# Masks of two groups of columns in one VectorE operation, in a graph attention layer with a 0/1 adjacency matrix

## The reference

```python
xt = jnp.einsum('ni,hio->hno', x, W)
src = jnp.einsum('hnf,hf->hn', xt, a[:, :out_f])
dst = jnp.einsum('hnf,hf->hn', xt, a[:, out_f:])
e = jax.nn.leaky_relu(src[:, :, None] + dst[:, None, :], 0.2)
e = jnp.where((adj_matrix > 0)[None, :, :], e, -jnp.inf)
h_prime = jnp.einsum('hij,hjf->hif', jax.nn.softmax(e, axis=2), xt)
x = _layernorm(x + h_prime.transpose(1, 0, 2).reshape(n, heads * out_f), axis=-1)
```

## Time and profile before

| what | value |
|---|---|
| median of 3 runs | 2133.12 us (2133.09 to 2134.42) |
| span of the profiled execution | 2129.9 us |
| TensorE matmul busy | 2068.3 us, 97% |
| VectorE busy | 2037.9 us, 96% |
| ScalarE busy | 1991.4 us, 93% |
| chain that ended last | TensorE 85%, ScalarE 7%, VectorE 4% |

### The profile page before, as it was taken

One profiled execution on the slowest core, in us unless ns is written; L12 is line 12 of the kernel. 1 busy time (PEld: TensorE's weight loads), 2 busy tenths in 40 slices (PEclk: granted clock), 3 DMA queues, 4 the chain that ended last, 5 costly groups with the idle time before them and its releaser, 6 DMA issues.

```text
span 2129.9 us, 76758 instructions
## 1 busy us (share of the span) xinstructions
PE 2068.3 (97%) x34256; PEld 2045.3 (96%) x34256; DVE 2037.9 (96%) x2147; ACT 1991.4 (93%) x2019; POOL 203.9 (10%) x179
## 2 busy tenths in 40 slices
PE   7779999999999999999999999999999999999997
PEld 5569999999999999999999999999999999999997
DVE  4999999999999999999999999999999999999887
ACT  4588999999999999999999999999999999999995
POOL 0200000000200102000020002001020001201000
PEclk9999999999999999999999999999999999999998
DMA  9999777666666766676666766767666766534321
GB/s 309 372 368 383 270 259 251 228 216 212 212 219 220 260 219 216 206 245 221 218 218 218 260 217 196 230 212 255 216 219 216 246 224 215 185 83 122 87 53 41
DMA packets 237208, 469.37 MB, mean 220 GB/s; under 512 B 14736, under 2 KB 23952, under 8 KB 236880
## 3 DMA queue, kind: packets, MB, share of 16 engines
q1 hardware_dynamic: 232672, 448.58, 63.9%
q0 software_dynamic: 4080, 15.73, 2.2%
q10 hardware_dynamic: 128, 0.13, 0.0%
HBM read 438.83 MB, written 25.56 MB: 218 GB/s over the span
## 4 chain that ended last, share of the span: by engine, by line
PE 85%; ACT 7%; DVE 4%; DMA 1%; issue 1%; SPq 0%; POOL 0%; DVEq 0%; ACTq 0%; POOLq 0%
PE acc L997 80%; ACT big L504 7%; PE tp L961 4%; DVE AT L679 1%; DVE big L684 1%; DVE big L686 1%; DVE AT L678 1%; PE acc L913 0%; DMA AT<-in_x_dram 0%; DMA raw<-in_adj_dram 0%; PE acc L923 0%; DMA v_parts<-big 0%; DVE nat L624 0%; SPq L321 0%; PE tp L951 0%
## 5 line engine op out<-in xcount | busy, mean ns | idle before, releaser
L504 ACT ACTIVATE big<-big,d_all 128x1024 int8<-128x1024 f32 x1776 | 1872.4, 1143 | 36.7 <-PE acc L997 36.6
L997 PE MATMUL acc<-big 128*128 128x130 f16 x32768 | 1889.1, 220 | 8.8 <-DVE big L708 7.9
L997 PEld LDWEIGHTS acc<-big 128*128 128x128 fp8e5 x32768 | 1878.0, 98 | 11.7 <-issue 10.3
L701 DVE SCALAR_TENSOR_TENSOR big<-big,AT 128x1024 uint32<-128x1024 uint32 x512 | 625.5, 1222 | 26.3 <-ACT big L504 24.5
L708 DVE SCALAR_TENSOR_TENSOR big<-AT,big 128x1024 uint32<-128x1024 uint32 x512 | 625.1, 1221 | 3.0
L693 DVE TENSOR_SCALAR big<-big,d_all 128x1024 uint8<-128x1024 f32 x272 | 204.6, 752 | 0.0
L624 DVE TENSOR_SCALAR nat<-raw 128x2048 fp8e4<-128x2048 int32 x128 | 176.7, 1381 | 2.9 <-DMA raw<-in_adj_dram 2.6
L626 DVE TENSOR_SCALAR nat<-raw 128x2048 uint8<-128x2048 int32 x128 | 177.5, 1387 | 0.0
L439 POOL TENSOR_TENSOR wden<-big,ab 128x16 f32<-128x16 f32 x31 | 68.3, 2205 | 885.0 <-DVE big L734 885.0
L635 DVE SCALAR_TENSOR_TENSOR AT<-AT,tp 128x1024 uint32<-128x1024 uint32 x112 | 136.4, 1217 | 0.1
L961 PE MATMUL tp<-ident,nat 128*128 128x128 f32 x896 | 116.8, 273 | 0.0
(11 more groups left out here) (67 smaller groups left out, 403.1 us busy)
## 6 DMA issues: line engine op xcount, KB each, us to landing
raw<-in_adj_dram SPq DMA_DIRECT2D x256, 1024.0 KB, 6.2
big<-v_parts SPq DMA_DIRECT2D x512, 260.0 KB, 3.6
v_parts<-big SPq DMA_DIRECT2D x16, 1040.0 KB, 6.1
big<-s_rows SPq DMA_DIRECT2D x32, 512.0 KB, 4.5
AT<-in_x_dram SPq DMA_DIRECT2D x16, 512.0 KB, 8.9
big<-in_x_dram POOLq DMA_DIRECT2D x8, 1024.0 KB, 8.0
out_dram<-big POOLq DMA_DIRECT2D x7, 1024.0 KB, 5.9
out_dram<-big SPq DMA_DIRECT2D x2, 384.0 KB, 2.7
```

The source lines that it names most:

```text
L504: return nc.scalar.activation(sgn[:, g % NB, b, :], srow[:, h % 2, :], ACT.Sign, bias=dflat[:, r:r + 1], scale=-1.0)
L701: nc.vector.scalar_tensor_tensor(out=word(sgn, g % NB), in0=word(sgn, g % NB), scalar=EDGE[plane], in1=edges(g), op0=ALU.bitwise_and, op1= ...
L997: return nc.tensor.matmul(acc[:, k, o:o + 2 * VO], m[:, g % NB, b, t * P:(t + 1) * P], Vr[:, v:v + 2 * VO], start=opens, stop=False, skip_ ...
```

## The change

In all passes but the first, the positive masks of groups g and g + 1 (g even) are made by one operation over 2048 words instead of two over 1024, and so are the negative masks. Both stand at the even group. The compares of both groups come ahead of the pair's positive masks, and converts stay at the odd group, which is now behind the pair's negative masks. The merge waits for the positive masks of the pair just issued and for the negative masks of all pairs before.

```diff
+            def masks_of_two(n, g, plane, cmps, kept):
+                for k in kept:
+                    dve.wait_ge(at_done, k)
+                dve.wait_ge(cmp_done, cmps)
+                dve.wait_ge(sgn_done, n + 2)
+                of = words_of(sgn, g % NB)
+                nc.vector.scalar_tensor_tensor(out=of, in0=of, scalar=EDGE[plane], in1=edges_of(g),
+                                               op0=ALU.bitwise_and, op1=ALU.bitwise_and).then_inc(pos_done, 2)
+
+            def rest_of_two(n, g, plane, kept):
+                for k in kept:
+                    dve.wait_ge(at_done, k)
+                dve.wait_ge(sums_done, n + 2)
+                dve.wait_ge(pos_done, n + 2)
+                nc.vector.scalar_tensor_tensor(out=words_of(neg, g % NB), in0=edges_of(g), scalar=EDGE[plane], in1=words_of(sgn, g % NB),
+                                               op0=ALU.bitwise_and, op1=ALU.bitwise_xor).then_inc(neg_done, 2)
...
-                z = (g - j) % NG
-                dve.wait_ge(pos_done if z == 0 else neg_done, n + 1 if z == 0 else n - z + 5)
+                dve.wait_ge(pos_done, n - n % 2 + 2)
+                dve.wait_ge(neg_done, n + 4 + n % 2)
...
-                        if not made:
-                            masks_of(n, g, plane, (0 if first else compared_ahead(c)) + compared(g, h, first, not more), last[g])
+                        single = first and h == 0
+                        ahead = 0 if first else compared_ahead(c)
+                        if single and not made:
+                            masks_of(n, g, plane, ahead + compared(g, h, first, not more), last[g])
+                        if not single and g % 2 == 0:
+                            if scalar_blocks(g, first, not more) < B:
+                                compares(n, g, h, scalar_blocks(g, first, not more))
+                            if scalar_blocks(g + 1, first, not more) < B:
+                                compares(n + 1, g + 1, h, scalar_blocks(g + 1, first, not more))
+                            masks_of_two(n, g, plane, ahead + compared(g + 1, h, first, not more), (last[g], last[g + 1]))
                         if ended and g == 1:
                             high(p, 0)
-                        by_scalar = scalar_blocks((g + 1) % NG, first and h > 0, not more)
-                        if by_scalar < B and not made:
+                        by_scalar = scalar_blocks((g + 1) % NG)
+                        if single and by_scalar < B and not made:
                             compares(n + 1, g + 1, h, by_scalar)
...
-                        if not made:
+                        if single and not made:
                             rest_of(n, g, plane, last[g])
+                        if not single and g % 2 == 0:
+                            rest_of_two(n, g, plane, (last[g], last[g + 1]))
```

More of the change, by code:

```diff
@@ L185, in word, with words_of, edges_of @@
             return t[:, n].rearrange("p b i -> p (b i)").bitcast(u32)
+        def words_of(t, n):
+            return t[:, n:n + 2].rearrange("p n b i -> p (n b i)").bitcast(u32)
+        def edges_of(g):
+            return AT[:, g:g + 2].rearrange("p g b s i -> p (g b s i)")
         def edges(g):
```

## The result

The changed kernel takes 2278.47 us (median of 4 runs, 2274.31 to 2280.29), against 2133.11 beside it: 1.068 of the time before (1.0668 to 1.0694). The prediction was 2225, with 2178 to 2250 as its range; the direction was right, and the time lies 53 us above the forecast and 28 above the range. The profiled execution spans 2277.8 us instead of 2129.9, so 147.9 us are to be explained.

What follows compares the result with a forecast made beforehand. TensorE was taken as the floor, its steady passes without gaps. Stalls of 3.2 us in 24 passes (77), 6 in the last four and 9 in passes 1 to 3 sum to 92: from 2133.1 to 2225 us, range 2178 to 2250.

Steps and rivals of the forecast that it cites:

- it can't overlap by 0.09 and starts 0.03 after its end: VectorE's masks or merge directly behind the masks they wait for: 0.12 us each, seven times a pass, 0.8 us.
- Three such pairs: 1.1 us a pass.: Pairs with a merge at groups 6, 10 and 14: TensorE stands 0.38 us at each one's first negative mask.
- Rival A: The merge pairs just fit, with 0.1 less in each hiding their stall; 2.1 us a pass, 2198 us; chance 0.17.
- "0.6 us" where a pass begins: Group 0: the first high, now behind the double masks, lets TensorE start at 12.97 against arrival at 12.36.
- Groups 2 and 3, "1.5 us": The lows hold back these signs: negative masks usable at 23.52, wanted at 22.05, so TensorE stands 1.5 us.
- Passes 1 to 3, "9, from 3 to 14": ScalarE itself is the chain there; about 2 us stall where a pass begins, few long loops; 3 us a pass.
- "Sum 6" for the last passes: Last four passes: 0.6 us entering pass 28, then 1.9 at each later beginning, 5.7 together; other pairs in time.

Runs made afterwards that it cites:

- e1: The changed kernel with a pair's compares moved ahead of the convert before them, away from the masks; 2265.38 us, 1.0622 of before.
- e5: e1, with the merge no longer waiting for the pair just issued where it doesn't touch it; 2238.62 us, 1.0496 of before.
- e11: The kernel before, with even groups' positive masks also waiting for the odd group's signs, from group 2 and pass 4 on; 2166.31 us, 1.016.
- e13: e11 with the operation that weighs the sums (group 8) cut to 1 column of 64; 2166.25 us, 1.0153 of before.
- e17: The kernel before, with only group 14's positive mask also waiting for group 15's signs, from pass 4 on; 2156.93 us, 1.0115.
- e18: e11 with the two adds at group 12 cut to 1 column of 64; 2157.31 us, 1.0116 of before.
- e12: The changed kernel with single masks in passes 0 to 3 and at groups 0 and 1 of every pass; 2249.45 us, 1.0545 of before.
- e4: The changed kernel with single masks in the whole first chunk (passes 0 to 3), pairs from pass 4 on; 2251.15 us, 1.0554 of before.
- e3: The changed kernel with a pair's negative masks again two operations, one behind the other at the same place; 2264.98 us, 1.062 of before.
- e9: e8 with the pairing left out in passes 1 to 3 and at groups 0 and 1 of every pass; 2156.04 us, 1.0111 of before.
- e10: The changed kernel with compares ahead of the convert, merge at the odd group, single masks in passes 0 to 3 and groups 0 to 3; 2181.11 us, 1.0229.
- e8: The kernel before, with only a pair's negative masks made in one operation, at the odd group ahead of the convert; 2191.84 us, 1.0277.

## Why the prediction was wrong, by its own steps

Sign and places were right: five stalls a pass, at the first `high` and at groups 2, 6, 10 and 14, the double mask at 2.29 us (2.28 predicted), VectorE's busy time unchanged. Sizes were not. The sum was 92 us and 147.9 were measured: 21 of the 56 missing lie in passes 1 to 3, 29 in passes 4 to 27, 6 at the end. Two things failed in the steady passes: the price of a wait of VectorE for itself, and the lateness that one pair hands to the next, which stood in the sum as nothing.

*"it can't overlap by 0.09 and starts 0.03 after its end".* The loss of overlap was right, the 0.03 was mis-sized. Rows 7 are of operations on 6 and 3 elements a partition; for the merge behind a double mask it is 0.20, for a mask behind a mask 0.13. With 0.17 more for the merge the working comes out right where nothing else is late: at group 6 it gives 0.38 + 0.17 = 0.55, and 0.39 + 0.16 = 0.55 were measured. A wait of 0.23 behind the compares, which the change puts right ahead of the masks, wasn't in the sum. Taken off, the compares' waits give back 13 us (e1) and the merges' 27 (e5), thereof 10 and 24 in passes 4 to 27. Of the 24, 0.12 x 4 x 24 = 11.5 were in the sum.

*"Three such pairs: 1.1 us a pass."* 0.39 + 0.52 + 0.71 and three times 0.16: 2.1. The growth from 6 to 14 is the queue: 0.13 and 0.33 us beyond the signs, by the table above, so 0.55 + 0.13 = 0.68 and 0.55 + 0.33 = 0.88, as measured (0.52 + 0.16 and 0.71 + 0.16). The working took each pair for itself, and excludes this. Rival A, a loop 0.1 shorter that just fits, had the sign of the error wrong.

*"0.6 us" where a pass begins.* The working starts the masks 0.15 us behind the last sign. They started 1.0 behind (1084.27 to 1085.29), since VectorE was still at the work of the pair before and at the compares. The stall was 1.07 + 0.16 instead of 0.6; that it didn't grow by the whole 0.9 is because TensorE came later too, by the larger stall at group 14 (0.87 instead of 0.38). e11, e13, e17 and e18 show this mechanism apart: the slack of a pair isn't its own, and late work is passed on down the queue.

*Groups 2 and 3, "1.5 us".* 1.14 + 0.16 = 1.30. This one was smaller, since TensorE came later to it, by the larger stall ahead of it. e1 and e12 show the trade: what is taken from one shows at the other.

*Passes 1 to 3, "9, from 3 to 14".* 30.0, of which 2.4 came ahead of the change; e4 says 27. This is the largest miss of one term. The working expected 2 us where a pass begins and few long loops; there were stalls of 4.45, 2.07, 0.70 and 1.67 us at the four beginnings and seven more inside. It put no convert between the two masks, and it took TensorE's clock as constant.

*"Sum 6" for the last passes.* 12.1. The stalls between them were 1.68 to 1.96 us, as predicted (1.9); behind two of them the clock fell, 1.6 us each, and a stall of 0.45 that wasn't in the sum stands in each of two passes. Pass 28 begins with 0.75 + 0.16 instead of 0.6.

```profile
2072.08 5.71 PE L1030 MATMUL acc<-big 128*128 128x130 f16 x96 [0.45 <-DVE big L731]
2079.47 31.25 PE L1030 MATMUL acc<-big 128*128 128x130 f16 x544 [1.68 <-DVE big L757]
2111.17 27.63 PE L1030 MATMUL acc<-big 128*128 128x130 f16 x480 [0.45 <-DVE big L731]
2140.76 60.01 PE L1030 MATMUL acc<-big 128*128 128x130 f16 x1024 [1.96 <-DVE big L757]
```

Two readings in the prediction are off by a hundredth or a tenth, without a consequence: single masks start 1.14 apart, not 1.13 (1022.26 to 1023.40), and the signs of a pair's first group end at 4.5, not 4.4 (0.24 + 3 x 1.04 + 1.14).

The Trainium skill says ("Perfetto Trace Analysis", Optimizing Scalar/DVE Operations) that grouping and performing larger operations can improve throughput if the engine is saturated. Here VectorE was busy for 98.7% of the steady passes, and grouping its masks made the kernel 6.8% slower. The same section says that where these engines aren't saturated but cause bubbles on others, breaking up instructions may allow work to be completed sooner. That agrees with the changed kernel, where VectorE is busy for 89% of the span and 120.6 us of TensorE's idle time stand ahead of its sums: breaking up the negative masks again gained 13 us (e3), breaking up all masks 145 (the kernel before).

What stays open: what is left in e9 (23 us) and e10 (48 us) was read from timelines and not taken apart further. In passes 4 to 27 the queue's direct part is 1.2 of 4.45 us a pass; how the rest divides between the wait for signs and the length of the masks, no run separates in the changed kernel, and these parts don't simply add up, as stalls hand time to one another. None of the versions beat the kernel before, whose matmuls have no gap in these passes to give back.

## What to carry to other kernels

Here an operation over two units of work starts when its last input is there, and the next engine gets the first result when all of it is done (2.29 us later). In a pipeline in which the engine that bounds has no gaps, that is paid at each place without slack, and the saved overhead (0.07 us a mask) isn't on the path. To price a late operation, follow the queue behind it, without a gap, to the next thing that another engine waits for, some ten operations and the next pass if need be (e17); slack that was counted for each pair alone is counted several times. Take the price of an operation that waits for its direct predecessor from rows of the same kind and size (0.13 to 0.23 us here, against 0.03 between operations on a few elements), and count each such pair of neighbours that an edit creates.

## What the runs showed of the hardware

A stall of TensorE can cost more than its length. In e3, behind the stall of 2.15 us, the granted clock was 0.50 (1.2 GHz) for about 3.4 us. TensorE's timeline, then busy times in windows of 1 us (the third number from the end is the granted clock):

```profile
1015.05 12.72 PE L1031 MATMUL acc<-big 128*128 128x130 f16 x192 [2.15 <-DVE big L757]
```

```profile
1017.00:1018.00 1.00, 1.00 (x13) 1.00 (x11) 0.63 (x1) 0.98 (x1) 0.60 (x2) 0.50 0.56 199
...
1020.00:1021.00 1.00, 1.00 (x21) 1.00 (x19) 0.80 (x2) 0.44 (x1) 0.00 (x0) 1.00 1.04 408
```

The 192 matmuls took 12.72 us instead of 11.15 to 11.36 as in e8 and e11, some 1.6 us more. In the changed kernel it happened behind four stalls: where pass 1 begins, where 64 matmuls took 6.52 us instead of 3.90, where pass 2 begins (a stall of 2.07), and behind both stalls of 1.96 near the end.

```profile
214.28 6.52 PE L1030 MATMUL acc<-big 128*128 128x130 f16 x64 [4.45 <-DVE big L757]
```

It didn't behind the stall of 1.68, nor behind one of 2.27 in pass 3. In e3's passes 4 to 27 TensorE stands for 2.15 us (or 2.14) at twelve beginnings and for 1.82 (or 1.81) at the other twelve; the clock fell behind six of the first kind and none of the second. In e12 it fell behind four of six stalls of 1.93 us and none of seventeen of 1.65. What decides between stalls of one length these runs don't show. The four stretches cost some 7 us of the 147.9 in the changed kernel (2.6 and three times 1.6), and those of e3's passes 4 to 27 some 9.
